# An attention and sparse-expert block on one core: dispatch rows without the attention result, adding scatters at the end

## What is computed

```python
xn = layernorm(x)
# attention, causal and linear, per sequence
z = layernorm(xn)                      # here folded into one scale and shift of x
q, k, v = split(z @ qkv_w + qkv_b)     # gain and bias folded into the weights
k = elu(k * sigmoid(z @ gate_w + gate_b)) + 1;  q = elu(q) + 1
att = ((q @ k.T) * tril) @ v / (sum(q * cumsum(k)) + eps)
# experts: 8 of them, each token takes its best 2 of a Sinkhorn-balanced router
gates = sinkhorn((xn @ router_w.T + router_b) / temperature)
y = sum over the 2 chosen experts e of gate_e * ((relu(xn @ wg[e]) * (xn @ wp[e])) @ wo[e])
out = x + att + xn + y
```

## Time and profile before

| | us |
|---|---|
| three timed executions | 433.36, 436.21, 438.42 |
| their median | 436.21 |
| span of the profiled execution (first to last instruction) | 365.3 |
| median less that span | 70.9 |

### The profile page before, as it was taken

The page is one execution under the profiler, slowest core; times in us unless marked ns, Lnnn a source line. Parts: engine busy times, 40 slices in busy tenths (PEclk is TensorE's granted clock), DMA queues, the critical chain, the costliest instruction groups (busy, mean ns, idle before and its releaser), DMA issues.

```text
span 365.3 us, 8755 instructions
## 1 busy us (share of the span) xinstructions
PE 331.2 (91%) x2560; PEld 301.9 (83%) x2560; DVE 268.4 (73%) x726; ACT 236.1 (65%) x437; POOL 268.1 (73%) x364
## 2 busy tenths in 40 slices
PE   0788989879999999998999999999999999999980
PEld 0678748647888888876999999999899999999970
DVE  3898889998988888887576676567666667667640
ACT  2669854323767667566777775788677777777530
POOL 3496999975777776557577777777777777777773
PEclk9999999987999999999999999999999999999995
DMA  6999999999344342348599987617665565572110
GB/s 172 255 295 336 333 334 307 290 297 275 121 145 146 105 145 89 117 115 249 164 318 377 346 246 203 173 54 194 187 196 158 151 172 164 150 225 74 50 39 5
DMA packets 64189, 70.97 MB, mean 194 GB/s; under 512 B 6002, under 2 KB 59006, under 8 KB 64144
## 3 DMA queue, kind: packets, MB, share of 16 engines
q1 hardware_dynamic: 54016, 48.70, 49.0%
q0 software_dynamic: 8672, 21.19, 16.0%
q10 hardware_dynamic: 1456, 0.53, 0.7%
HBM read 28.54 MB, written 43.04 MB: 196 GB/s over the span
## 4 chain that ended last, share of the span: by engine, by line
PE 75%; DVE 12%; DMA 3%; issue 3%; POOL 2%; SPq 2%; ACT 2%; POOLq 0%; ACTq 0%; DVEq 0%
PE psum L1765 17%; PE psum L1750 8%; PE psum L1752 8%; PE psum L1751 8%; PE psum L1572 4%; PE psum L1654 4%; PE psum L1636 4%; DMA rows<-in_L_attn_x 3%; PE psum L1463 3%; PE psum L1516 2%; POOL out L614 2%; PE psum L1740 2%; PE psum L1554 2%; PE psum L1557 2%; PE psum L1519 2%
## 5 line engine op out<-in xcount | busy, mean ns | idle before, releaser
L592 POOL DMA_INDIRECT by_lower<-rows,slot_u x64 | 64.4, 1006 | 28.7 <-issue 18.4
L614 POOL DMA_INDIRECT out<-rows x70 | 68.9, 985 | 21.4 <-issue 16.5
L1750 PE MATMUL psum<-xT_high,w_now 128*128 128x256 f32 x256 | 77.1, 301 | 1.9 <-DVE xT_low L1387 1.1
L1765 PE MATMUL psum<-w_expert,hT 128*128 x560 | 75.4, 276 | 1.0 <-DVE hT L1396 0.7
L825 ACT ACTIVATE w_now<-w_split 128x1024 fp32r x63 | 66.7, 1059 | 14.7 <-PE psum L1752 14.7
L1751 PE MATMUL psum<-xT_low,w_now 128*128 128x256 f32 x256 | 71.6, 280 | 0.0
L1752 PE MATMUL psum<-xT_high,w_now 128*128 128x256 f32 x256 | 71.5, 279 | 0.0
L603 POOL DMA_INDIRECT by_upper<-rows x58 | 57.2, 987 | 17.7 <-issue 11.6
L1400 DVE TENSOR_TENSOR hT<-relu,psum 128x512 f32<-128x512 f32 x64 | 44.0, 688 | 35.5 <-ACT relu L844 18.0
L1765 PEld LDWEIGHTS psum<-w_expert,hT 128*128 128x128 f32 x560 | 68.7, 191 | 1.4 <-issue 1.3
L844 ACT ACTIVATE relu<-psum 128x512 f32<-128x512 f32 x64 | 38.2, 598 | 22.0 <-PE psum L1752 21.9
(11 more groups left out here) (277 smaller groups left out, 660.3 us busy)
## 6 DMA issues: line engine op xcount, KB each, us to landing
by_lower<-blank SPq DMA_DIRECT2D x1, 10140.0 KB, 34.4
by_upper<-blank SPq DMA_DIRECT2D x1, 10062.0 KB
rows<-by_upper SPq DMA_DIRECT2D x32, 258.0 KB, 3.0
rows<-by_lower SPq DMA_DIRECT2D x26, 260.0 KB, 4.3
rows<-in_L_attn_x SPq DMA_DIRECT2D x8, 512.0 KB, 9.8
lead_row<-by_lower SPq DMA_DIRECT2D x6, 260.0 KB
out<-rows POOLq DMA_INDIRECT x70, 2.5
w_expert<-in_L_ffn_wg SPq DMA_DIRECT2D x8, 128.0 KB, 2.5
```

What stands on the lines that cost most here:

```text
L592: pool.indirect_dma_start(by_lower, bass.IndirectOffsetOnAxis(ap=slot_u[:, t:t + 1], axis=0), rows[:, t, :], None)\
L614: pool.indirect_dma_start(out_rows, bass.IndirectOffsetOnAxis(ap=row(n)[:, k, TOKEN:TOKEN + 1].bitcast(U32), axis=0), row(n)[:, k, BASE], ...
L1750: pe.matmul(target, high, x_high, start=True, stop=False)
L1765: last = pe.matmul(psum[:, 4 + n % 2, k * D:(k + 1) * D], hT[:, n % 3, f, k * P:(k + 1) * P], weights, start=(f == 0), stop=(f == FB - 1))
```

## The change

The dispatch row is cut to Z, GATE_UP, TOKEN, GATE_LOW, SLOT_UP (132 columns, 528 bytes), and the wait for `row_done` ahead of each scatter is gone. SP stores BASE plus attention in token order into the last 8192 rows of the output, 16 DMAs of 4 tiles: 13 among the expert weight loads, the last 3 ahead of the loads of entries 6, 7 and 8. The load of entry 6 waits for the 10 stores that read the ring's tiles. In the first pass `save_y` writes gate times product with no addition; in the second it adds that first part. The second pass's scatters add to the output (`compute_op=ALU.add`), without a bounds check. The output tensor becomes 17152 rows; its first 8960 are a place for the empty places' rows: `aside` gives each a row number of its own, and an instruction more per entry of the second pass takes the maximum of it and the token number. `turn_row(0)` and `turn_row(1)` are put ahead of the last group's `add_state`/`out_chunk`, into banks 1 and 2.

```diff
-            count_up(blank[:, TOKEN:TOKEN + 1].bitcast(U32), [[1, 1]], NOWHERE)
+            count_up(aside[:], [[P, TILES_OUT]], 0, 1)
...
+            def store_group(n):
+                sp.wait_ge(row_done, (n + 1) * G)
+                at = OUT_AT + n * GW
+                sp.dma_start(out[at:at + GW, :].rearrange("(g p) d -> p g d", p=P),
+                             rows[:, n * G:(n + 1) * G, BASE]).then_inc(early_stored if n < RING_GROUPS else late_stored, 16)
...
                 if n == LEAD:
                     sp.wait_ge(scattered, 16 * NT)
+                    sp.wait_ge(early_stored, 16 * RING_GROUPS)
...
+            for n in range(NG - 3):
+                for e in range(1, E - 1):
+                    if FREED_BY[e] == n:
+                        sp.wait_ge(o_ready, n + 1)
+                        load_expert(e)
+                store_group(n)
             for e in range(1, E - 1):
-                sp.wait_ge(o_ready, FREED_BY[e] + 1)
-                load_expert(e)
+                if FREED_BY[e] >= NG - 3:
+                    sp.wait_ge(o_ready, FREED_BY[e] + 1)
+                    load_expert(e)
...
             for n in range(LEAD, NE):
+                if LEAD <= n < LEAD + 3:
+                    store_group(NG - 3 + n - LEAD)
...
                     if t == SOON:
                         pool.wait_ge(scattered, 16 * SOON)
-                    pool.wait_ge(row_done, t + 1)
                     pool.indirect_dma_start(by_lower, bass.IndirectOffsetOnAxis(ap=slot_u[:, t:t + 1], axis=0),
-                                            rows[:, t, :], None)\
+                                            rows[:, t, LOWER], None)\
...
+            pool.wait_ge(early_stored, 16 * RING_GROUPS)
+            pool.wait_ge(late_stored, 16 * (NG - RING_GROUPS))
             for n in range(NE, 2 * NE):
...
-                    pool.indirect_dma_start(out_rows, bass.IndirectOffsetOnAxis(
+                    pool.indirect_dma_start(out, bass.IndirectOffsetOnAxis(
                         ap=row(n)[:, k, TOKEN:TOKEN + 1].bitcast(U32), axis=0),
-                        row(n)[:, k, BASE], None, bounds_check=last_token, oob_is_err=False)\
+                        row(n)[:, k, BASE], None, compute_op=ALU.add)\
...
             def save_y(n):
+                if n >= NE:
+                    at = tiles_before(n) - tiles_before(NE)
+                    token = row(n)[:, 0:width(n), TOKEN].bitcast(U32)
+                    dve.tensor_tensor(token, token, aside[:, at:at + width(n)], ALU.max)
...
+                    if n < NE:
+                        dve.tensor_scalar(target, product, row(n)[:, k, GATE_LOW:GATE_LOW + 1], None, ALU.mult)\
+                           .then_inc(y_saved, 1)
+                    else:
+                        dve.scalar_tensor_tensor(target, product, row(n)[:, k, GATE_UP:GATE_UP + 1], target,
+                                                 ALU.mult, ALU.add).then_inc(y_saved, 1)
...
                 if not ahead:
+                    turn_row(0)
+                    turn_row(1)
                     for c in range(G):
                         add_state(n, c)
                         out_chunk(n, c)
-                    turn_row(0)
-                    turn_row(1)
                     continue
```

More of the change, by code:

```diff
@@ L20, with rows_out @@
 BIG = 4.0
+EXPERTS = 8
+def rows_out(tokens):
+    return 2 * tokens + (EXPERTS - 2) * 128
 def sparse_block_kernel(nc, x, qkv_w, qkv_b, gate_w, gate_b, ln_g, ln_b,
@@ L45, in sparse_block_kernel @@
     NE = PAIRS + SINGLES
+    TILES_OUT = 2 * PAIRS + SINGLES
+    OUT_AT = TILES_OUT * P
     MIXED = NE - FULL
@@ L57, in sparse_block_kernel @@
     ROW_UP, ROW = 2 * D + 2, 2 * D + 4
+    LOWER, UPPER = slice(D, ROW), slice(0, ROW_UP)
     NOWHERE = 2 * NBLOCK * W
@@ L61, in sparse_block_kernel @@
     W_EXPERT = DOWN.stop
-    assert 2 * NB <= NT and D == P and C == 8 and GB == 2 and FB == 2 and K * NT <= 512
+    assert out.shape[0] == OUT_AT + NTOK and 2 * NB <= NT and D == P and C == 8 and GB == 2 and FB == 2 and K * NT <= 512
     x_view = x.rearrange("b (c p) d -> b p c d", p=P)
-    out_rows = out.rearrange("b t d -> (b t) d")
-    by_lower = nc.dram_tensor("by_lower", ((NBLOCK + 1) * W, ROW), F32).ap()
+    by_lower = nc.dram_tensor("by_lower", ((NBLOCK + 1) * W, ROW - D), F32).ap()
     by_upper = nc.dram_tensor("by_upper", ((NBLOCK + 1) * W, ROW_UP), F32).ap()
@@ L267, in sparse_block_kernel @@
         x_in = [sem(f"x_in{b}") for b in range(B)]
-        (v_loaded, w_loaded, const_ready, lower_cleared, upper_cleared, scattered) = steps(
-            "v_loaded w_loaded const_ready lower_cleared upper_cleared scattered")
+        (v_loaded, w_loaded, const_ready, lower_cleared, upper_cleared, scattered, early_stored, late_stored) = steps(
+            "v_loaded w_loaded const_ready lower_cleared upper_cleared scattered early_stored late_stored")
         (rw_loaded, rw_pe, rw_step, w_scaled, w_summed, w_sum_saved, w_step) = steps(
@@ L367, in turned_to @@
             if n < 2:
-                return psum[:, FIRST_BANKS[n], 0:W]
+                return psum[:, 1 + n, 0:W]
             return psum[:, 6 + n % 2, 0:W]
@@ L433, in load_row @@
                         sp.wait_ge(row_out[m % NB], GONE_LAST)
-                sp.dma_start(row(n)[:, 0:tiles, 0:columns],
+                sp.dma_start(row(n)[:, 0:tiles, columns],
                              source.rearrange("(t p) r -> p t r", p=P)[:, bass.ds(first, tiles), :]).then_inc(row_in[q], 16)
+            for n in range(NG - 3):
[4 more added lines that the diff above has]
+                store_group(n)
             for e in range(1, E - 1):
-                sp.wait_ge(o_ready, FREED_BY[e] + 1)
-                load_expert(e)
+                if FREED_BY[e] >= NG - 3:
+                    sp.wait_ge(o_ready, FREED_BY[e] + 1)
+                    load_expert(e)
             sp.wait_ge(route_dve, TABLES_STEP)
             for n in range(LEAD):
-                load_row(n, by_lower, ROW)
+                load_row(n, by_lower, LOWER)
             for n in range(LEAD, NE):
+                if LEAD <= n < LEAD + 3:
+                    store_group(NG - 3 + n - LEAD)
                 if n == LEAD + 4:
@@ L450, in _ @@
                     load_expert(E - 1)
-                load_row(n, by_lower, ROW)
+                load_row(n, by_lower, LOWER)
             for n in range(NE, 2 * NE):
-                load_row(n, by_upper, ROW_UP)
+                load_row(n, by_upper, UPPER)
             for n in range(2 * NE - NB, 2 * NE):
@@ L475, in _ @@
             count_up(class_no[:], [[1, K]], 0)
-            count_up(rows[:, :, TOKEN].bitcast(U32), [[P, NT]], 0, 1)
+            count_up(rows[:, :, TOKEN].bitcast(U32), [[P, NT]], OUT_AT, 1)
             pool.memset(blank[:], 0.0).then_inc(const_ready, 1)
@@ L604, in _ @@
                         ap=row(n)[:, k, SLOT_UP:SLOT_UP + 1].bitcast(U32), axis=0),
-                        row(n)[:, k, 0:ROW_UP], None, bounds_check=last_upper, oob_is_err=False)\
+                        row(n)[:, k, UPPER], None, bounds_check=last_upper, oob_is_err=False)\
                         .then_inc(row_out[q], 16)
@@ L1806 @@
         args.append(nc.dram_tensor("in_" + name, a.shape, mybir.dt.from_np(a.dtype), kind="ExternalInput").ap())
-    shape = arrays["in_L0_attn_x"].shape
-    out = nc.dram_tensor("out", shape, F32, kind="ExternalOutput").ap()
+    b, t, d = arrays["in_L0_attn_x"].shape
+    out = nc.dram_tensor("out", (rows_out(b * t), d), F32, kind="ExternalOutput").ap()
     sparse_block_kernel(nc, *args, out)
     r = run_bass_kernel_spmd(nc, [arrays], core_ids=[0])
-    return r.results[0]["out"]
+    return r.results[0]["out"][-b * t:].reshape(b, t, d)
```

14 lines of the change are left out of this document (5 added, 9 removed).

## The result

The changed kernel takes 512.31 us (median of 4 runs, 507.39 to 515.13), the kernel before 437.31 beside it (433.36 to 442.4): ratio 1.174, 95% interval 1.1668 to 1.1811. The prediction was 437, in a range of 432 to 457. The timed executions of one kernel fall into a faster and a slower group, some per cent apart, and every ratio here compares the faster groups, so it need not be the quotient of the medians beside it.

What follows compares the result with a forecast made beforehand. POOL's 140 scatters were taken to bound phase two, PE, ACT and DVE's chain phase one. Terms 0.3 − 0.07 + 0.2 + 0 + 0.8 = +1.2 us on span 365.3 gave 366.5; plus 70.9: 437.4, rounded to 437, range 432 to 457.

Steps and rivals of the forecast that it cites:

- Dispatch without the wait: Dispatch in phase one: last scatter starts near 171.5 instead of 175.83, but nobody is helped; value 0.
- rival E: Dispatch: may still be paced otherwise, ending at 171 even with no wait, making that half idle; expected, no separate chance given.
- The median stands 70.9 above that span, and nothing I see in the change moves what lies around it.: Outside the profiled span of 365.3 us: 70.9 us carried over unchanged onto the predicted span of 366.5.
- POOL's list of 140 scatters sets the end: Phase two: from its first scatter POOL, at 1.291 us a step, sets the end, 3.35 us behind DVE's last addition.
- The nearest row is the other added step per row ... at 0.022; I take this.: Second pass's adding scatters: adding priced like the bounds check, 0.022 us each over 70, +1.5 us.
- Rival A: Second pass: adding scatter dearer on POOL by d, end moves 70 d; 441 to 471 us, middle 451; chance 0.32.
- Unchecked scatters: Second pass's 70 scatters: no bounds check saves 0.022 us each, −1.5 us, given back by the adding.
- Stores and half the bytes: 0.: SP's 16 stores, and fewer bytes in clearing, dispatch and first loads: nothing waits for them, each valued 0.
- turn_row, bounds 0 and 2.2, I take 0.3.: PE ahead of the last attention group: moved transposes save nothing but may wait for entry 1's landing; +0.3 us.
- save_y −0.07, maxima +0.2.: DVE: first-pass multiplication at a copy's 0.28 us, −0.07; 38 second-pass maxima may lengthen POOL's scatters, +0.2 us.
- Landing +0.8: End of the kernel: last adding scatters read rows first and the last tile is real rows; +0.8 us, bounds 0 and 4.7.
- Rival B: Second pass: adding scatters' transfers become the bound, pacing POOL's list; 459 us at 1.6 us per step; chance 0.05.

Runs made afterwards that it cites:

- wait_back: The changed kernel with the wait for `row_done` put back ahead of each dispatch scatter: 455.43 us, ratio 1.0477.
- plain_out: The changed kernel without `compute_op` on the last scatters, so they overwrite the stored attention rows: 491.87 us, ratio 1.1316.
- both_back: The changed kernel with the dispatch wait back and plain last scatters, leaving attention's rows out of the output: 448.11 us, ratio 1.0177.
- both_back2: both_back run again on another chip, beside turn_back: 446.64 us, ratio 1.0043.
- before_again: The kernel before, word for word, timed and profiled again: 434.67 us, ratio 0.996, span 432.3.
- no_stores: The changed kernel without SP's sixteen stores and the waits on them, so base and attention miss the output: 513.06 us, ratio 1.1803.
- turn_back: both_back2 with `turn_row` of entries 0 and 1 back behind the last attention group, in before's banks: 448.36 us, ratio 1.013.
- paced4: The changed kernel with every fourth dispatch scatter waiting until all scatters before it have landed: 447.95 us, ratio 1.0188.
- add_dispatch: The changed kernel with `compute_op` add on the dispatch scatters too, no wait; read up to phase two's start: 467.09 us, ratio 1.0623.
- before_pace4: The kernel before with every fourth dispatch scatter first waiting for all earlier ones to land, ahead of its attention wait: 437.17 us beside 436.07.
- pass_pace: before_pace4 plus, in both passes, a wait ahead of each second pair for the two previous pairs to land: 470.72 us, ratio 1.0808.

## Why the prediction was wrong

The loss has two parts, in times: before 436, with the missing wait alone +57 (after less wait_back), with the addition +20 (after less plain_out), which makes 513 against 512.31 measured; both undone gives 1.0043 to 1.018 of before. The second term is the less certain: taken from wait_back's ratio (1.0477) less those of both_back and both_back2, it is 13 to 19 us.

- **"Dispatch without the wait", "Value 0, and no bound above that ...".** This step failed, and by itself it made the prediction wrong. I reckoned what POOL would gain and who would be helped, and gave no bound below zero. The wait was also a pause of POOL, and attention lived on it. With the wait gone phase two starts at 257.95 us, and with it back at 198.29. Nothing in the profile given showed this: PE was busy 29.71 of 30 us there while POOL issued the same first run of scatters. What would have hinted at it was the next point. That dispatch would go in an even row from 87 to 172 came true within 2 us; rival E took just this row for a sign that the edit was idle.
- **"The median stands 70.9 above that span, and nothing I see in the change moves what lies around it."** Failed. A span 16% shorter than the times is not an offset to carry over; the profiled execution was another kind of run than the timed ones. In the profiles of after and of all fifteen experiments 1.7 to 1.8 us lie outside the span. For the same reason "POOL's list of 140 scatters sets the end" holds for the given profile only: in before_again POOL waits 35.7 us for DVE ahead of the scatters of the second pass. The test I had named (a time outside the span that differs from 70.9) fell at once: 1.7.
- **"The nearest row is the other added step per row ... at 0.022; I take this."** Mis-sized: the term of +1.5 for adding. Measured are 1.560 − 0.957 = 0.60 us a scatter, 42 us over 70 on POOL's list, above even the upper bound of 0.48. The Trainium skill calls descriptor generation "small, variable" ("DMA: Bandwidth & Descriptors", section "Anatomy of one DMA — SWDGE (gpsimd) path"), and by that rule an adding scatter would have been as short as a plain one; the 0.60 us do not bear this out. No run shows what they are spent on.
- **Rival A.** Its place and kind were right: in the second pass POOL is 1.86 us a step and nothing else limits. By its rule 70 d is 42 us; in time it is about 20, since the plain scatters it is measured against have a cost of their own that the adding ones lack (32.3 us of waits for DVE in plain_out, 7.5 in after).
- **Unchecked scatters**, −0.022 each: right, 0.957 to 0.968 against 0.985.
- **Stores and half the bytes: 0.** Right as far as can be told: no_stores is not faster, and both_back2, which has both, is within 1% of before.
- **turn_row, bounds 0 and 2.2, I take 0.3.** Within what can be told: turn_back is not faster.
- **save_y −0.07, maxima +0.2.** The multiplication from PSUM took 0.345 us, not the 0.28 of a copy, so that saving was not there. The 38 maxima took 0.152 to 0.156 us as read from the earlier trace rows. Both are lost in the sum.
- **Landing +0.8.** From the start of the last scatter to the span's end it is 6.51 us in after and 6.38 before (365.3 − 358.92), with 0.58 of it the longer scatter: no added landing is seen.
- **Rival B** fell: between adding scatters the gap is 0.30 in 57 steps (17.4 us of "issue" in the group), the other 13 wait for DVE, and the DMA share is 0.72.

What stays open: by what path POOL's plain scatters delay what ACT and DVE take from PE, why adding ones don't, and why one execution of the kernel before was free of it. The trace names no releaser but `remote`, an unknown queue. These idle times are the mark by which the stages can be sorted. There are none in any stage of the given profile, none in the adding dispatch of add_dispatch, and none in the second pass of after, wait_back, no_stores, paced4 and add_dispatch, where the scatters add. Beside plain scatters they come to 85.4 us in the dispatch of after, 32.0 in that of before_again, 5.3 in paced4's and 0 in before_pace4's. The passes of the kernel before bear the same mark (24.9 and 24.6 us), and take 117.66 and 112.53 us where they took 90.43 and 88.98 in the given profile. That it is the same cause there is likely and not shown: the pauses of pass_pace did not remove it. A pause by computing alone, of a microsecond or more, was not tried, nor were plain scatters at a step of 1.85 us.

## What to carry to other kernels

A wait that looks idle can be the pause on which other engines run: before taking it away, ask what its engine will do without a stop, and, where that is a long unbroken run of indirect scatters from POOL, try a pause in every few of them. In dispatch every fourth was enough; in the passes, where POOL stopped by itself, more pauses only cost time. Set span against time before anything else: where they are far apart, the profiled execution is not the one being timed, and its busy shares and waits describe another run. An accumulate on a DMA that sits on the critical list is to be priced by a measurement of its own, not by the nearest plain one.

## What the runs showed of the hardware that I had not expected

- Plain indirect scatters of 128 rows, issued by POOL every 1.26 us without a pause, let PE, DVE and ACT start almost nothing: 1.66 of 30 us of PE busy at a DMA share of 0.16. What is late are ACT and DVE instructions behind a matmul (up to 19.7 us after it has ended); the steps from ACT to PE and to DVE stay at 0.03 to 0.10 us. In after it sets in within the first ten scatters (PE still had 14.17 of 16 us in 84:100) and ends some microseconds behind the last.
- A pause of 1.6 us or more after every fourth is enough (29.08 of 30 in 130:160); three in 64 are not (0.67 of 30); a memset of 0.12 us between scatters is not (7.65 of 30).
- Adding scatters, at 1.85 us, do not do it: 29.71 of 30 in the same stretch at a DMA share of 0.65.
- An adding scatter of 128 rows occupies POOL for 1.56 us, a plain one for 0.96, whether its rows are 512 bytes (the last pass) or those of dispatch (1.55).
- One kernel had executions of 365 us of span and of 432 with the same instructions; every timed execution was of the longer kind.
